# The second routing of a mixture-of-experts kernel: one expert's weights loaded earlier, two low parts moved on TensorE, eight lane tiles made by ACT

## Time and profile before

| | us |
|---|---|
| median of three runs | 955.72 |
| lowest and highest | 954.75, 956.1 |
| the profiled execution | 951.11 |
| its span, first to last instruction | 949.3 |
| PE busy in the span | 875.8 (92%) |
| DVE, ACT, POOL busy | 568.0, 487.4, 431.6 |

### The profile page before, as it was taken

How to read it: one execution, slowest core, us unless ns; L and a number is a source line. 1 busy time by engine, 2 the same in 40 slices (tenths; PEclk the granted TensorE clock), 3 DMA queues, 4 the chain that set the end, 5 groups by cost and what they waited for, 6 DMA issues and landing times.

```text
span 949.3 us, 19403 instructions
## 1 busy us (share of the span) xinstructions
PE 875.8 (92%) x6172; PEld 751.9 (79%) x6173; DVE 568.0 (60%) x1292; ACT 487.4 (51%) x1038; POOL 431.6 (45%) x374
## 2 busy tenths in 40 slices
PE   5899999867999998679999999997899999999995
PEld 4698989746899997457777777765599999999994
DVE  7885463485666667566666666687654545445442
ACT  5744231255444453466576665565454554555542
POOL 2473432004555573667264463320444555656532
PEclk9999999978999999899999999997899999999998
DMA  9731000175766755761020000328377667667662
GB/s 308 238 105 41 5 1 1 55 251 175 272 231 232 253 189 168 173 159 48 1 68 23 19 27 1 117 77 273 126 213 213 194 196 208 190 209 203 187 198 27
DMA packets 68609, 134.72 MB, mean 142 GB/s; under 512 B 8096, under 2 KB 50720, under 8 KB 63424
## 3 DMA queue, kind: packets, MB, share of 16 engines
q1 hardware_dynamic: 55200, 110.27, 34.3%
q0 software_dynamic: 13344, 23.63, 11.2%
HBM read 109.08 MB, written 21.64 MB: 138 GB/s over the span
## 4 chain that ended last, share of the span: by engine, by line
PE 63%; DMA 5%; DVE 4%; POOL 3%; issue 2%; ACT 2%; SPq 0%; POOLq 0%; DVEq 0%; ACTq 0%
PE d_hps L1995 15%; PE d_yps L2005 7%; PE b_hps L1995 7%; PE c_av L1022 5%; PE c_tp L1010 5%; PE c_sc L997 4%; PE c_xb L946 4%; PE d_yps L2008 4%; PE b_yps L2005 3%; PE b_yps L2008 2%; PE c_xb L1031 1%; DMA d_w<-in_w 1%; PE c_xb L969 1%; DMA x<-k_rows 1%; PE d_take L1984 1%
## 5 line engine op out<-in xcount | busy, mean ns | idle before, releaser
L1892 ACT ACTIVATE x<-d_hps,b 128x128 f32<-128x128 f32 x312 | 89.2, 368 | 120.5 <-PE d_hps L1995 119.4
L1995 PEld LDWEIGHTS d_hps<-d_xg_t,d_xw 128*128 128x128 f32 x1248 | 147.8, 195 | 1.4
L1995 PE MATMUL d_hps<-d_xg_t,d_xw 128*128 128x128 f32 x1248 | 148.0, 278 | 0.0
L905 POOL TENSOR_SCALAR c_prob<-c_prob,c_rinv 128x1024 f32<-128x1024 f32 x64 | 72.3, 1146 | 108.0 <-DVE c_rinv L1365 107.6
L2005 PE MATMUL d_yps<-d_w,d_hid_hi 128*128 x312 | 115.2, 402 | 0.0
L1802 POOL DMA_INDIRECT out_x<-d_y,d_take_slot x39 | 63.2, 1619 | 99.4 <-DVE d_y L2220 92.5
L1358 DVE CUSTOM_DVE_ANT_0 c_prob<-c_sc,c_minf 128x1024 f32<-128x1024 f32 x64 | 75.7, 1219 | 29.0 <-PE c_sc L997 26.8
L2183 DVE TENSOR_SCALAR d_xg_t<-d_take,ln_w,ln_b 128x128 f32<-128x128 f32 x78 | 28.5, 406 | 92.0 <-PE d_take L1984 91.9
L2008 PE MATMUL d_yps<-d_w,d_hid_lo 128*128 x312 | 81.2, 281 | 0.0
L1010 PE MATMUL c_tp<-const,c_prob 128*128 128x128 f32 x512 | 70.6, 281 | 10.6 <-DVE c_pt L1370 5.2
L1995 PEld LDWEIGHTS b_hps<-b_xg_t,b_w 128*128 128x128 f32 x624 | 76.7, 195 | 2.9 <-issue 1.3
(11 more groups left out here) (370 smaller groups left out, 2063.1 us busy)
## 6 DMA issues: line engine op xcount, KB each, us to landing
d_xw<-in_w SPq DMA_DIRECT2D x39, 1024.0 KB
b_w<-in_w SPq DMA_DIRECT2D x47, 512.0 KB, 3.6
d_w<-in_w SPq DMA_DIRECT2D x8, 1024.0 KB, 8.3
a_raw<-in_ctx_t SPq DMA_DIRECT2D x8, 512.0 KB, 7.2
a_raw<-in_ctx SPq DMA_DIRECT2D x8, 512.0 KB, 4.4
ybuf<-a_zero SPq DMA_DIRECT2D x2, 2048.0 KB, 12.6
k_stage<-in_ctx_t SPq DMA_DIRECT2D x12, 256.0 KB, 3.1
rows<-b_xn_all SPq DMA_DIRECT2D x1, 2048.0 KB, 12.4
```

Of the source, the lines that this page charges most:

```text
L905: nc.gpsimd.tensor_scalar(prob[w][:], prob[w][:], rinv[:, w:w + 1], 1.0, ALU.mult, ALU.mult).then_inc(s["prob_ready"], 1)
L1892: op = nc.scalar.activation(hid[q][:, h * FH + c, :], src[:, c, :], ACT.Gelu_apprx_tanh, bias=b1[:, ds(e, 1), h * FH + c])
L1995: mm = nc.tensor.matmul(hps[j % 2][h][:, c * P:(c + 1) * P], w1[j % WL][:, k, at:at + P], xg_t[j % 2][:, k, :], start=(k == 0), stop=(k == ...
```

## The change

- Weights: `w2` of expert five is loaded with expert four's (`FREE_FIRST = (4, 5)`). For that `prob` and `v` exchange their places in SBUF, so that expert five's region lies over keys and `prob[0]`, `prob[1]`, and SP also waits until the transposes of unit six of the last batch are done (`tp_hi`). Six and seven stay in `LAST_LOW`.
- Casts: expert five's stands behind the fifth copy of turned tiles (`HIGH_AT = (2, 4)`).
- Turns: the last two pairs are turned in the usual order, two pairs ahead of the logits.
- Low parts by PE: expert six's four chunks stand ahead of the rank matmuls, expert seven's behind the slots matmuls; four warm matmuls instead of eight follow. ACT empties expert six's chunks ahead of the exponential, and expert seven's behind the value copy and the lanes.
- Lanes: ACT makes eight of the 32 lane one-hots, as in the first routing.

```
@@ -33,8 +33,8 @@
 LANES = 3
 EARLY_LOW = (2, 3)
 LATER_LOW = (0, 1)
-FREE_FIRST = 4
-LAST_LOW = (5, 6, 7)
+FREE_FIRST = (4, 5)
+LAST_LOW = (6, 7)
 ROUTED = {n: k + 1 for k, n in enumerate("load exp_in expert blk val slot g gate_at".split())}
 ACT_ROUTED = {n: k + 1 for k, n in enumerate("exp_ready val0_ready off_ready lane_act".split())}
 HIGH_ORDER = (0, 1, 4, 5, 6, 7)
@@ -750,8 +750,8 @@
         sb("gap", [P, 5248])
         q_hi, q_lo = (sb(f"q_{p}", [P, KD, S], F32R) for p in ("hi", "lo"))
         k_hi, k_lo = (sb(f"k_{p}", [P, KD, M], F32R) for p in ("hi", "lo"))
+        prob = [sb(f"prob{q}", [P, M]) for q in range(4)]
         v = sb("v", [P, JC, H, HD])
-        prob = [sb(f"prob{q}", [P, M]) for q in range(4)]
         pt = [sb(f"pt{q}", [P, JC, S]) for q in range(2)]
         att_t = sb("att_t", [P, KD, S])
         att_odd = sb("att_odd", [P, 2 * P])
@@ -882,7 +882,9 @@
             out_rows(B - 2)
             sp.dma_start(dram["out"][T * P:(T + 1) * P, :], m.x[:, 0, :]).then_inc(m.out_ready, 16)
             sp.wait_ge(s["max_done"], B * UP * 2)
-            m.load_w2(sp, FREE_FIRST)
+            sp.wait_ge(s["tp_hi"], B * UP * 2 - 2)
+            for n in FREE_FIRST:
+                m.load_w2(sp, n)
             m.early_rows(sp)
             sp.wait_ge(s["av_done"], B * 4)
             for n in LAST_LOW:
@@ -1537,8 +1539,8 @@
     XN_OUT = 32 if first else 48
     LAST = slice(T - TB, T)
     DVE_LOW, PE_LOW, DVE_LAST = ((0, 1, 2, 3), (4, 5), (6, 7)) if first else ((LATER_LOW[1], 4), (6, 7), (5,))
-    HIGH_AT = (1, 3, 5, 7) if first else (2, 5)
-    LANES_ACT = 8 if first else 0
+    HIGH_AT = (1, 3, 5, 7) if first else (2, 4)
+    LANES_ACT = 8
     CH = FC // 2
     STEPS = 6
     tag = "b_" if first else "d_"
@@ -1846,6 +1848,8 @@
                     high(act, (0, 1, 2, 3)[HIGH_AT.index(i)] if first else HIGH_AT.index(i) + 4)
             for e in PE_LOW:
                 high(act, e)
+            if not first:
+                low_out(PE_LOW[0])
             act.wait_ge(s["routed"], ROUTED["exp_in"])
             nc.scalar.activation(e2[:], dlog[:], ACT.Exp).then_inc(s["act_routed"], 1)
             def value_parts():
@@ -1863,10 +1867,13 @@
                 nc.scalar.activation(in_lane[:, tail, :], off, ACT.Relu, scale=-1.0,
                                      bias=m.const[:, C_ONES:C_ONES + 1]).then_inc(s["act_routed"], 1)
 
-            for e in PE_LOW:
-                low_out(e)
-                if e == PE_LOW[1 if first else 0]:
-                    value_parts()
+            if first:
+                for e in PE_LOW:
+                    low_out(e)
+                value_parts()
+            else:
+                value_parts()
+                low_out(PE_LOW[1])
             if first:
                 for e in DVE_LAST:
                     high(act, e)
@@ -1950,20 +1957,20 @@
                 turn_pair(i)
             pe.wait_ge(s["w_in"], 32)
             for i in range(PAIRS):
-                if i + AHEAD < (PAIRS if first else PAIRS - AHEAD):
+                if i + AHEAD < PAIRS:
                     turn_pair(i + AHEAD)
-                if not first and i == PAIRS - AHEAD:
-                    for late in range(i, PAIRS):
-                        turn_pair(late)
                 logits(i)
                 warm(1, rank)
 
+            if not first:
+                low_parts(PE_LOW[0])
             pe.wait_ge(s["routed"], ROUTED["load"])
             nc.tensor.matmul(rank[:, 0:E * T], c16(C_ONES, P), load[:], start=True, stop=True)
             nc.tensor.matmul(rank[:, E * T:2 * E * T], c16(C_BEFORE, P), load[:],
                              start=True, stop=True).then_inc(s["pe_routed"], 1)
-            for e in PE_LOW:
-                low_parts(e)
+            if first:
+                for e in PE_LOW:
+                    low_parts(e)
 
             pe.wait_ge(s["routed"], ROUTED["val"])
             pe.wait_ge(s["act_routed"], ACT_ROUTED["val0_ready"])
@@ -1975,7 +1982,9 @@
                 mm = nc.tensor.matmul(slots[:, 0:2 * NBX], in_lane[:, n, :], val[:, n, :, :].rearrange("p a b -> p (a b)"),
                                       start=(n == 0), stop=(n == 2 * T - 1))
             mm.then_inc(s["pe_routed"], 1)
-            warm(8, rank)
+            if not first:
+                low_parts(PE_LOW[1])
+            warm(8 if first else 4, rank)
 
             def turn_in(n, j, turn):
                 pe.wait_ge(gathered[j % GATHERS], turn(j, GATHERS) * 16 + 16)
```

## The result

| | before | changed |
|---|---|---|
| median of the first three runs, us | 955.72 | 949.33 |
| lowest, highest | 954.75, 956.1 | 948.92, 950.24 |
| profiled execution, its span | 951.11, 949.3 | 949.33, 947.6 |

The ratio is 0.9944 (95% interval 0.9927 to 0.9962): 6.4 us less by the medians, where the forecast was 1.3 less and the range ended at 951.6. The two profiles differ by 1.78 us only.

The account below looks back on a forecast made before the run. It took PE as the limit in the second expert layer, and the chain of waits through the second routing ahead of it. Gains of 0.5 + 0.59 + 0.24 = 1.3 us gave 955.72 - 1.3 = 954.4 us, range 951.6 to 956.9.

Parts of the forecast that it names:

- step 4: Slots end to third block, expert seven's low part there: ups start 2.26 us later, run 2.50 shorter; net 0.24 gained.
- the step that carried the median over: The median shown lies 4.61 us above the profiled execution; this was kept, so 955.72 - 1.3 = 954.4.
- Step 1: Second routing's logits: expert five loaded early and usual order of tiles let the logits end 2.35 us earlier.
- Step 2: Expert six's low part before the rank matmuls: rank ends at 658.8, 0.5 us gained; bounds 1.1 gained, 1.1 lost.
- Step 3: Rank end to slots end, now 13.99 us: DVE makes 24 lanes, ACT eight; 0.59 us gained, bounds 0.59 and 0.95.
- Sum: Gains of 0.5, 0.59 and 0.24 make 1.3 us, taken off the median of before: 954.4 us.
- The first, that the clock stays up: PE never idles until the rank, clock rises soon after slots: 1.1 + 0.59 + 2.5 = 4.2 us gained, 951.5; chance 0.22.
- The slower rival: Rank matmuls wait behind ACT's cast of expert seven: 0.9 to 3.3 us slower, deciding from rank end 660.1; chance 0.13.

Follow-up runs that it names:

- e3: Kernel of before with only expert five's load and cast early; late turns, both low parts after the rank and DVE's 32 lanes stay: ratio to before 0.9983.
- e9: Kernel of before with only the usual order of turns; expert five's load and cast stay late: ratio to before 1.0000.
- e5: Changed kernel with the last two pairs turned late again, behind the sixth pair's logits: ratio to before 1.0005, median 954.61 us.
- e11: Changed kernel with late turns and three warm matmuls instead of one behind the logits of pairs 3, 4 and 5: ratio to before 0.9987.
- e13: Changed kernel, unchanged, run once more in a later series: ratio to before 0.9973.
- e2: Changed kernel, unchanged, measured again in a longer series: ratio to before 0.9969.
- e1: Kernel of before, unchanged, measured again: ratio to before 0.9991.
- e15: Kernel of before, unchanged, one more profile: 67.09 us from the attention's last score matmul to the second layer's first down matmul.
- e8: Kernel of before with expert five loaded and cast early and the usual order of turns, nothing else: ratio to before 0.9953.
- e10: Kernel of before with early load and cast of expert five, usual turns, and 22 warm matmuls instead of 8 behind the slots: ratio to before 0.9943.

## Why the prediction was wrong

It had the direction right and the size wrong. Of the 5.1 us between the forecast of 954.4 and the result of 949.33, some 1.8 lie in the stretch that the steps cost, above all in step 4, and 3.2 in the step that carried the median over. By its own steps:

- *Step 1.* Between the two profiles it is right to 0.01 us: first turn to the end of the logits 13.75 before, 11.39 after, 2.36 less. The changed side holds in all ten profiles with the early load and the usual turns (10.58 or 10.59 us to the last logits). What was thin is the base, one execution: from the first turn to the rank the three other profiles of before took 0.7 to 1.7 us longer. I read the warm logits of the earlier trace rows as their fixed price, put the gain down to the load's wait and priced the order of turns as the same work in another order. e3 and e9 show that neither gives it alone, and e3, e5 and e11 why: with the last turns late the logits could lose the clock, and then the wait that the load took away came back as slow matmuls.
- *Step 2.* Expert seven's load took the second place in the queue and chunk three waited for ACT, as written. The rank end came 17.70 us after the first turn, 18.74 before: 1.04 gained where I took 0.5. Both ends of the bounds exist: e13 lost the clock in the last logits, before the chunks. That the point where the clock changes differs between runs of one kernel is what the Trainium skill says ("TensorE: Matmul & The Clock Gate", "Part 1: The HAM clock gate"); the profiles of the changed kernel agree: 6.89, 7.08 and 8.75 us to the rank.
- *Step 3.* 13.47 us for 13.99: 0.52 gained, 0.59 forecast.
- *Step 4.* The mis-sized term: 1.59 us gained, 0.24 forecast. I carried the 6.91 us that four chunks took from a long idle time over to chunks that stand directly behind slots matmuls; here they took 5.53, the first alone at the lower pace, and the register load of 0.46 was not to be seen. The exchange that it described, a later start for ups at the full clock, is right: 7.41 for 7.14 expected.
- *Sum.* 3.15 us between the profiles for 1.33. The other 3.2 us of the first result came from the step "median shown is 4.61 above that profile, which I carry over". So half of the first result was the luck of three executions, as the longer series show. The spread of single executions, 950 to 959 in before, is larger than all terms of the sum; a median of three of each moves by a microsecond or two of itself (the ten of e2 have a standard deviation of 2.3), and the range had no room for that.
- *Rivals.* The first, that the clock stays up (951.5), was nearest: two of its three terms nearly came in (1.04 for 1.1, 0.52 for 0.59), the third with 1.59 for 2.5. The slower rival's place was real: 1.20 us of waiting, and in e13 a rank that started 19.33 us after the first turn, 0.92 later than in the first profile of before. That passes its point of decision (0.83), yet S was 1.5 us shorter than in that profile, because step 4 gave more than forecast; and in e1 and e15 of before the rank came later still, at 20.14 and 20.15.

## What to carry to other kernels

When work is moved on TensorE, ask what stands between the small matmuls that stay. Here, with the transposes of the last pairs moved away from between them, the logits lost the clock in the fifth or sixth pair in four of six profiles, though the engine was busy up to there; with the transposes between them and the load early, in none of ten. Ahead of a burst that waits for a transfer, try warm matmuls in the idle time before rearranging real work: here 14 of them took a microsecond off the burst. And read a base from several profiles where its executions spread wider than the gain that is looked for.

## What the runs showed of the hardware

A TensorE that is busy for all of 2 us ran at 0.62 and then 0.50 of its clock (e3), the lower of the two levels. It fell while PE did logits of eight columns with one warm matmul behind each pair's. With 0.4 us of transposes ahead of each pair's logits (e8), or with three warm matmuls instead of one (e11), it stayed at 1.00. The runs do not separate what it is in the added work that held the clock. Ahead of the first turn of gathered rows PE was idle for 3.29 us in before, and the ups began at 0.50; in e10 it was idle for 0.73 us there and kept 1.00.
